# A recurrent branch run as a front stage, or in tiles of 128 tokens inside the last layer and the drain

## The reference, cut to what matters

```python
# recurrent branch, 192 hidden channels
u = xn @ W_in.T
gate, xh = split(u)                          # 192 and 192
xh = causal depthwise convolution, 4 taps
forget, inp = split(xh @ W_gates + b_gates)
alpha = exp(-8 * softplus(forget_base) * sigmoid(forget))
beta  = sqrt(1 - alpha**2 + 1e-6)
h[t]  = alpha[t] * h[t-1] + beta * sigmoid(inp) * xh
branch = (gelu(gate) * h) @ W_out.T

# six layers, 16 heads of 64, windows of 32 tokens, then a gated feed-forward part
y = xn
for l in range(6):
    y = y + local_attention(y)
    y = y + ffn(layernorm(y))

out = x + silu(y) * branch
```

## Time and profile before

| | |
|---|---|
| Time, median of 3 runs | 1779.33 us (1776.90 to 1779.72) |
| The profiled execution: its time | 1778.04 us |
| its span in the profile | 1776.1 us |
| share busy: PE, DVE, ACT, POOL | 94%, 78%, 73%, 75% |
| mean granted clock of TensorE | 0.962 of full |

### The profile page before, as it was taken

How to read it: one execution, slowest core, us unless ns; L and a number is a source line. 1 busy time by engine, 2 the same in 40 slices (tenths; PEclk the granted TensorE clock), 3 DMA queues, 4 the chain that set the end, 5 groups by cost and what they waited for, 6 DMA issues and landing times. The chain is left out here.

```text
span 1776.1 us, 49117 instructions
## 1 busy us (share of the span) xinstructions
PE 1677.7 (94%) x19440; PEld 1352.5 (76%) x19440; DVE 1377.4 (78%) x1948; ACT 1290.9 (73%) x2317; POOL 1338.8 (75%) x1456
## 2 busy tenths in 40 slices
PE   5977899999999999999999999999999999999985
PEld 1114788878888878888878888878888878888874
DVE  8237888878888878888878888878888878888843
ACT  3314678778778788788788787787787787787874
POOL 4007888898888898888898888898888898888830
PEclk9557999999999999999999999999999999999997
DMA  4001332323432322432223333223333223223221
GB/s 127 0 7 57 95 97 80 98 66 93 118 108 67 93 85 80 113 109 80 80 85 92 101 109 95 69 81 107 89 106 96 86 63 108 82 81 91 83 61 51
DMA packets 179485, 150.47 MB, mean 85 GB/s; under 512 B 110782, under 2 KB 151484, under 8 KB 179132
## 3 DMA queue, kind: packets, MB, share of 16 engines
q1 hardware_dynamic: 179260, 147.34, 29.4%
HBM read 21.99 MB, written 1.05 MB: 13 GB/s over the span
## 5 line engine op out<-in xcount | busy, mean ns | idle before, releaser
L1310 POOL TENSOR_TENSOR qk<-qk,t 128x1024 f32<-128x1024 f32 x192 | 455.7, 2374 | 122.4 <-DVE qk L1130 121.0
L1127 DVE TENSOR_TENSOR t<-ps_qn,tab 128x512 f32<-128x512 f32 x384 | 265.2, 691 | 186.4 <-ACT sq L982 177.7
L1322 POOL TENSOR_TENSOR qkr<-qk,rinv 128x1024 f32<-128x1024 f32 x192 | 361.5, 1904 | 7.6 <-POOL rinv L1302 0.2
L769 PE MATMUL ps_qn<-w_hi,xs_hi 128*128 128x512 f32 x576 | 276.4, 480 | 15.5 <-POOL xs_lo L1359 9.0
L1018 ACT ACTIVATE qbd<-ps_tr 64x512 f32<-64x512 f32 x384 | 226.8, 591 | 86.1 <-PE ps_tr L795 81.4
L969 ACT ACTIVATE pbd<-ps_tr 64x512 f32<-64x512 f32 x384 | 226.0, 589 | 72.6 <-PE ps_tr L782 69.8
L982 ACT ACTIVATE sq<-ps_qn 128x512 f32<-128x512 f32 x384 | 228.8, 596 | 59.8 <-PE ps_qn L771 55.2
L1130 DVE TENSOR_TENSOR qk<-ps_qn,tab 128x512 f32<-128x512 f32 x384 | 261.4, 681 | 0.0
L771 PE MATMUL ps_qn<-w_hi,xs_lo 128*128 128x512 f32 x576 | 229.5, 398 | 0.0
L770 PE MATMUL ps_qn<-w_lo,xs_hi 128*128 128x512 f32 x576 | 228.9, 397 | 0.0
L1140 DVE TENSOR_REDUCE ss<-sq 128x32 f32<-128x2048 f32 x96 | 216.3, 2253 | 0.0
(11 more groups left out here) (144 smaller groups left out, 2998.3 us busy)
## 6 DMA issues: line engine op xcount, KB each, us to landing
v_own<-v_new SPq DMA_DIRECT2D x96, 512.0 KB, 3.3
v_back<-v_new SPq DMA_DIRECT2D x96, 384.0 KB, 3.6
v_back<-v_own SPq DMA_DIRECT2D x96, 128.0 KB, 2.3
kT<-kT SPq DMA_DIRECT2D x84, 128.0 KB, 2.9
w_raw<-in_Wqkv SPq DMA_DIRECT2D x18, 512.0 KB, 5.6
xsh<-x SPq DMA_DIRECT2D x192, 32.0 KB, 2.0
fx<-xmid SPq DMA_DIRECT2D x96, 64.0 KB, 2.1
wo<-in_Wo SPq DMA_DIRECT2D x6, 512.0 KB, 4.1
```

Of the source, the lines that this page charges most:

```text
L769: mm(ps_qn[bank][:, :], xs_hi[b][:, :], w_hi[:, part], start=True, stop=False)
L1127: v.tensor_tensor(t2[:, part].rearrange("p (h s d) -> p h s d", s=2, d=DH // 2), swapped, tab[:, 2 * k + 1:2 * k + 2, :].rearrange("p o (s ...
L1310: g.tensor_tensor(qk[b][:, part], qk[b][:, part], t2[:, part], ALU.add).then_inc(added[b], 1)
L1322: g.tensor_tensor(qkr[b][:, part].rearrange("p (h d) -> p h d", d=DH), qk[b][:, part].rearrange("p (h d) -> p h d", d=DH), rinv[b][:, k * ...
```

## The change

- The first stage is now `normalise`: it ends with the transposed rows in `x`. The branch's weights are no longer loaded there, and nothing of the branch is computed there.
- In step 1 SP copies `x` (1 MB) into `branch`, and loads `w_in` and the parameters. The copy keeps xn, since the layers overwrite `x`.
- In steps 40 to 47, half 1, PE adds the gate projection of one tile between `("up", 2)` and `("qkv", b, 5)`, in the same ring of two banks, and ACT its gelu.
- In the drain the rest of the branch runs in tiles of 128 tokens, both streams together (384 columns), at the end of each half. Tile k has four stages: projection and convolution; gates; scan; output. Stage s of tile k lies in drain half max(k-1, 0) + s, half 0 being (48, 0). Tile 7 ends in half 9, which is (52, 1).
- Both sigmoids are built as 1 / (1 + exp(-z)) with DVE's reciprocal on 128x384, the square root as exp(ln/2), so that ACT stays in one function table. Part of the element work goes to POOL.
- The branch's tiles lie in buffers of the layers that are free by then (`late` is the rotary table, `gate` is `w_raw`, others lie in `qk`, `t2`, `sq` and `v_new`). Their weights are loaded in (48, 0), once POOL has cleared `late`, with the combination's input behind them, as one DMA of 1 MB into `qk[0]`; `combine` loads nothing any more.
- The operation `pause` is gone, in all steps.

```diff
+def rec_tiles(i, b):
+    h = 2 * (i.n - STEPS) + b
+    return [[k for k in range(TILES) if max(k - 1, 0) + stage == h] for stage in range(4)]
...
+def rec_order(i, b):
+    hidden, gates, _, out = rec_tiles(i, b)
+    return ([("forget", k) for k in gates] + [("hidden", k) for k in hidden] + [("input", k) for k in gates]
+            + [("branch", k) for k in out])
...
-        order += [("up", 0), ("up", 1)] * up + [("qkv", b, 4)] * new + [("up", 2)] * up + [("qkv", b, 5)] * new
+        order += [("up", 0), ("up", 1)] * up + [("qkv", b, 4)] * new + [("up", 2)] * up
+        order += [("gate", i.tile)] * (b == 1 and new and i.n >= STEPS - TILES)
+        order += [("qkv", b, 5)] * new + rec_order(i, b)
...
+                def load_recurrent(i, b):
+                    if (i.n, b) == (1, 0):
+                        sp.dma_start(branch[:, :, :], x[:, :, 1:]).then_inc(branch_in, 16)
+                        sp.dma_start(rec.w_in[:, :], a["w_in_t"]).then_inc(rec_w, 16)
+                        sp.dma_start(rec.par[:, :, :], a["rec_par"]).then_inc(rec_par_in, 16)
+                    if (i.n, b) == (STEPS, 0):
+                        sp.wait_ge(rec_clear, 1)
+                        sp.dma_start(wg_lo, a["w_gates_t"][0:HID_LO, :]).then_inc(rec_wg, 16)
+                        sp.dma_start(wo_lo, a["w_out_t"][0:HID_LO, :]).then_inc(rec_wg, 16)
+                        for s in range(B):
+                            sp.dma_start(wg_hi[stream_rows(s), s, :], a["w_gates_t"][HID_LO:HIDDEN, :]).then_inc(rec_wg, 16)
+                            sp.dma_start(wo_hi[stream_rows(s), s, :], a["w_out_t"][HID_LO:HIDDEN, :]).then_inc(rec_wg, 16)
+                        sp.wait_ge(qk_ready[0], 2 * STEPS)
+                        sp.dma_start(w.tokens[:, :, :], a["x"].rearrange("b (t p) d -> p (b t) d", p=P)).then_inc(w.tokens_in, 16)
                 def half(i, b):
                     if b == 0:
                         shift_xmid(i)
+                    load_recurrent(i, b)
                     shift_x(*next_tile(i, b))
                     carry_k(i, b)
                     move_v(i, b)
...
+                def rec_from_conv(bank, k, c0):
+                    y, out = conv[k % len(conv)], ps_qn[bank]
+                    mm(out[:, 0:B * P].rearrange("p (b t) -> p b t", b=B), wg_lo[:, c0:c0 + HID_LO], y[:, 0:B, :], start=True, stop=False)
+                    for s in range(B):
+                        mm(out[:, s * P:(s + 1) * P], wg_hi[:, s, c0:c0 + HID_LO], y[:, 2, :], start=False, stop=(s == B - 1))
+                    for s in range(B):
+                        rows = stream_rows(s)
+                        mm(out[rows, B * P:3 * P], wg_lo[:, c0 + HID_LO:c0 + HIDDEN], y[:, s, :], start=True, stop=False)
+                        last = mm(out[rows, B * P:3 * P], wg_hi[:, s, c0 + HID_LO:c0 + HIDDEN], y[:, 2, :], start=False, stop=True)
+                    last.then_inc(qn_full[bank], 1)
...
                     scores(i, b)
+                    recurrent(i, b)
...
+                def recurrent(i, b):
+                    hidden_k, gates, scans, _ = rec_tiles(i, b)
+                    if 0 in hidden_k:
+                        decay_rates()
+                    for k in gates:
+                        e = decay[k % RING]
+                        wait_fill(dve, qn_done, qn_order, i, ("forget", k))
+                        v.tensor_scalar(e, e, 1.0, None, ALU.add).then_inc(rec_forget, 1)
+                        dve.wait_ge(rec_forget, 2 * k + 1)
+                        v.reciprocal(e, e).then_inc(rec_forget, 1)
+                    for k in hidden_k:
...
+                        for c in range(CONV_K):
+                            for pg, rows in ((0, slice(0, B)), (1, slice(B, 3))):
...
+                    for k in scans:
+                        e, z, h = decay[k % RING], drive[k % 2], state[k % 2]
+                        d = admit[k % RING]
+                        dve.wait_ge(rec_den, k + 1)
+                        v.reciprocal(d, d).then_inc(rec_div, 1)
+                        dve.wait_ge(rec_div, 2 * k + 1)
+                        dve.wait_ge(rec_drive, k + 1)
+                        v.tensor_tensor(z, z, d, ALU.mult).then_inc(rec_div, 1)
...
+                        for c in range(3):
+                            first = 0.0 if k == 0 else state[(k - 1) % 2][:, c, P - 1:P]
+                            v.tensor_tensor_scan(h[:, c, :], e[:, c, :], z[:, c, :], first, ALU.mult, ALU.add).then_inc(rec_h, 1)
...
+                def recurrent(i, b):
+                    hidden_k, gates, scans, _ = rec_tiles(i, b)
+                    if (i.n, b) == (STEPS - 1, 1):
+                        g.memset(late[:, 0:PADDED], 0.0).then_inc(rec_clear, 1)
...
+                        g.tensor_tensor(z, e, e, ALU.mult).then_inc(rec_var, 1)
+                        pool.wait_ge(rec_var, 2 * k + 1)
+                        g.tensor_scalar(z, z, -1.0, 1.0, ALU.mult, ALU.add).then_inc(rec_var, 1)
+                        d = admit[k % RING]
+                        wait_fill(pool, qn_done, qn_order, rec_step(k, 1), ("input", k))
+                        g.tensor_scalar(d, d, 1.0, None, ALU.add).then_inc(rec_den, 1)
+                        pool.wait_ge(rec_beta, k + 1)
+                        g.tensor_tensor(z, z, conv[k % len(conv)], ALU.mult).then_inc(rec_drive, 1)
+                    for k in scans:
+                        pool.wait_ge(rec_h, 3 * (k + 1))
+                        part = gate[:, :, token_tile(k)]
+                        g.tensor_tensor(part, part, state[k % 2], ALU.mult).then_inc(rec_gate, 1)
```

400 lines of the change are left out of this document (213 added, 187 removed).

## The result

The changed kernel takes 1790.56 us (median of 4 runs, 1788.33 to 1791.31) beside 1779.39 us of the kernel before on the same chip: ratio 1.0064, 95% interval 1.0046 to 1.0081. It is slower, where 1774 was forecast as faster. The range of 1752 to 1796 holds it.

The account below looks back on a forecast made before the run. PE was taken to bound the layers, a serial chain the front, and DVE's list the new drain. Terms -104.3 + 19.3 + 73.8 - 1.35 + 4 + 3 = -5.5 us gave 1774 us from 1779.33; range 1752 to 1796.

Parts of the forecast that it names:

- The front: Before the layers: their start falls from 128.88 to 24.6 us, set by POOL's splitting of the first weights; gain 104.3 us.
- normalising is over by 18.4 us: In the front: DVE and ACT end at 18.4 us and do not decide the layers' start; POOL's splits do.
- The last layer: Steps 40 to 47: PE's sixth chunk starts 2.4 us late, 0.9 work and 1.5 waiting for a bank; 19.3 us lost.
- the rival with a ring that costs nothing: Last layer: only the 0.9 us of gate matmuls is paid, 12 us less, 1762 us; chance 0.17.
- The drain: After the last layer: DVE's list with the branch's work lengthens it; loss 73.8 us, plus 4 for lock and 3 for clock.
- half by half on VectorE's list: In the drain: DVE's old and new work laid out per half on the old time axis, to 1834.7 us for 1760.9.
- a half (i, 1) first gets 3.9 us: In the drain: DVE frees a bank, PE makes the third feed-forward piece, ACT does gelu and table load; 14.1 us a half.
- The keys: Drain half (48, 0): the keys' carry, behind seven DMAs and 1 MB, lands some 4.5 us after ACT wanted it.
- The tail: Last tile, from POOL's product through PE's output, ACT, scan and product to the final copy: 8.5 us, to 1834.7 us.
- Clock and lock: In the drain: 3 us for PE at 1.2 GHz, 4 us for two-input SBUF DVE operations standing still while POOL works.
- TensorE as the bound: Rival: in the drain PE at 1.2 GHz needs 11.2 us a tile against DVE's 10.2; 1788 us, chance 0.22.
- The check written down: From the old 1691 us to the layers' end some 143 us where it was 69; wrong if under 120 or over 165.

Follow-up runs that it names:

- e8: Changed kernel with the three high halves of the first layer's weights rounded by ScalarE instead of GpSimd in the front: 1785.95 us.
- e1: Changed kernel with each tile's gate projection moved behind the scores, from ahead of the sixth projection chunk: 1788.39 us.
- e3: Changed kernel with GpSimd's product of gate and state moved into the next half, behind the newton steps and the diagonal: 1786.59 us.
- e13: Changed kernel with the forget base's first three small VectorE instructions moved to (47, 0) and ScalarE's exp to (47, 1): 1785.82 us.
- e2: Changed kernel with step 48's seven branch DMAs issued at the end of half (48, 0), behind the keys' carry: 1784.31 us.
- e14: Changed kernel with GpSimd's five branch instructions of each tile on one column instead of 128: 1782.18 us.
- e10: Changed kernel with twelve idle bf16 matmuls on TensorE at the start of each half from (50, 0) on: 1789.70 us.
- e16: Changed kernel with twelve idle bf16 matmuls in TensorE's wait ahead of the mask in (48, 1): 1788.44 us.
- e9: Changed kernel without the branch's matmuls on the padded upper halves of the gate and output weights: 1787.79 us.

## Why the prediction was wrong

- **The front**, 104.3 us forecast, 101.6 measured. The load and GpSimd's end were right. The step that failed is "normalising is over by 18.4 us": starting the splits earlier put them beside VectorE's scalings. The prediction described the lock between the two, counted only instructions with two tensor inputs as exposed, and applied it to the drain alone. The scalings read one tensor. Yet the trace of the kernel before had L309, with one tensor input and 2.20 us long beside GpSimd's difference. With less of GpSimd's work in the front (e8) the layers start 2.3 us earlier.
- **The last layer**, 19.3 us forecast, 19.4 measured. Right in size, in the place of the wait and in its releaser. e1 shows that the cost stays when the wait for the bank is gone, so the rival with a ring that costs nothing was no case, and the reason given for the 1.5 us explains where they are waited, not why they are lost.
- **The drain**, 80.8 us with its two shares, 97.8 measured; this is the step that gave the wrong sign. The sum of VectorE's work was right: 104 us in all for 81 and 22. What failed is "half by half on VectorE's list" with "a half (i, 1) first gets 3.9 us". The half (50, 1) takes 19.5 us for 14.1, since TensorE's broadcast waits for GpSimd's diagonal, and that for the scans by way of a product that stands ahead of it: 3 to 4 us by e3, where the next wait, 3.52 us for the bank, comes into view. (49, 1) takes 16.6 for 14.1; there ScalarE's copy `pbd`, behind the branch's ln and exp, holds TensorE; this is read off the trace, and no run tests it. The list of what is queued behind a waiting instruction was made for SyncE, TensorE and VectorE and left out GpSimd, whose work was only counted, and ScalarE. The rest of the list, forecast and measured: (48, 0) to its end at the maxima 16.7 and 18.8; (48, 1) 26.5 and 28.3, and from there to `take_out0` 6 and 8.5, in which together 2.9 us are the clock by the rows of e13; the rest of (49, 0) 14.5 and 17.8, of which 1.6 are a wait for ScalarE's exponential and 1.8 the lock on the convolution (3.86 us for 2.05); (50, 0), (51, 0) and (51, 1) 0.7, 1.0 and 1.4 us more. That is the whole overshoot: 24.7 us with the tail's 4.0, of which 7 had been set aside for lock and clock.
- **The keys** were in the forecast at 4.5 us and cost 6.3 (e2; 5.9 by the ratios), half by their later issue and half by the slower landing.
- **The tail**, 8.5 us forecast, 12.5 measured: GpSimd's adding one to the admission, one of its five instructions, holds VectorE's last reciprocal 3.24 us, again behind a product that waits for scans, and with GpSimd's work made small the tail is 2.7 us shorter (e14). TensorE runs it all at 1.2 GHz (the last row of the drain), which with idle matmuls ahead (e10, 0.82) is worth 0.9 us.
- **Clock and lock** were given 3 and 4 us. The clock costs 2 to 3 (e16, and the rows of e13). The lock costs some 5 us of VectorE's time in the drain (e14) and 2.3 in the front (e8). GpSimd's five instructions take 4.5 us a tile and not 3.5: adding one was taken at 0.5 us and takes 1.17, two of the products were taken at 0.83 and take 0.99.
- **The rivals.** TensorE as the bound gave 1788 us, and the measured 1790.6 is nearest to it; e9 and e10 show that the nearness is chance. The range held only because the rivals widened it.
- **The check written down**, 143 us from the old 1691 to the end of the layers and "wrong if over 165": 171, from VectorE's third `hid` of (47, 1) at 1604.00 to the combination at 1775.42. "DVE over 80% busy from (48, 1) on, and PE waiting for it" failed too: VectorE is busy 68% from the maxima at 1636.31 us on, and TensorE waits there 22.3 us for GpSimd, its longest wait of 9.68 us among them, and 15.5 for VectorE.

## What to carry to other kernels

When a chain is moved into another stage's lists, write down for every engine what of the old stage stands behind each new instruction that waits, for the engine that adds the least work too: here GpSimd's one product of 1 us, put ahead of a diagonal of 0.6 us, closed a loop over four engines. Sum of work on the busiest engine gives a lower bound of a drain, not its length: VectorE was idle for a third of it with the sum exactly right. And look at what an earlier start puts side by side: the splits and the scalings were harmless one after the other.

## What the runs showed of the hardware

- VectorE and GpSimd in SBUF: an instruction of two columns, 0.16 us alone, took 1.82 to 1.88 us beside GpSimd's 128x1024, with two tensor inputs (L1268) and with one (L1279, TENSOR_SCALAR). The sixteen 128x128 scalings with one tensor input went from 4.20 to 12.85 us. Reciprocals of 128x384 kept 2.50 to 2.55 us throughout the drain, beside GpSimd or not. The prediction had counted two-input instructions alone as exposed. The Trainium skill ("SBUF — State Buffer", § SBUF: two separate sides) names both, an operation in a two-port mode or with two SBUF inputs; the trace agrees for two inputs by L1268's 1.82 us. That an instruction with one tensor input is held as well is shown by L1279's 1.83 us and the scalings; that it is the two-port mode that makes it so, no run here shows.
- A reciprocal's price: 2 columns 0.17 us, 16 0.25 us, 384 2.55 us, so 6.3 ns a column holds from the two small ones to the wide one.
- A carry of 128 KB issued right behind a 1 MB load was waited for until some 8 us after its issue (1613.11 to 1621.3 us), where such a carry landed in 2.9 us in the median before the change. Sent ahead of the load it was waited for by nobody.
- The granted clock at the start of the layers is 1.00 over 27 to 55 us, where it had been 0.50 over 128 to 156 in the kernel before; ahead of the layers TensorE now does the transposes of the front with gaps of up to 1.95 us, at 1.00 over 12 to 27 us, where before it did the branch's output products from 111.18 to 127.2 us without a gap, at 0.50. Why the clock was low there although TensorE was busy, no run here tests. The start of the pipeline is 1.1 us shorter (first DMA to `take_out0` of step 5, 159.24 us for 160.31).
